# Rotary attention: which heads and queries one step takes, and how often its products are issued

## The reference, cut to what matters

```python
q = (x @ Wq + bq).reshape(B, S, H, Dh).transpose(0, 2, 1, 3)
k = (x @ Wk + bk).reshape(B, S, H, Dh).transpose(0, 2, 1, 3)
...
q, k = apply_rope(q, rope), apply_rope(k, rope)
attn = softmax(q @ k^T / sqrt(Dh))
out = (attn @ v) @ Wo + bo
```

## Time and profile before

| | before |
|---|---|
| median of 3 runs (lowest to highest) | 1888.64 us (1888.54 to 1892.25) |
| span of the profiled execution | 1890.9 us |
| PE busy | 1733.5 us (92%) |
| ACT busy | 1271.8 us (67%) |
| first to last start of an exponential of this layer | 1250.4 to 1777.8 us |

### The profile page before, as it was taken

The page is one execution under the profiler, slowest core; times in us unless marked ns, Lnnn a source line. Parts: engine busy times, 40 slices in busy tenths (PEclk is TensorE's granted clock), DMA queues, the critical chain, the costliest instruction groups (busy, mean ns, idle before and its releaser), DMA issues. The chain is left out here.

```text
span 1890.9 us, 25427 instructions
## 1 busy us (share of the span) xinstructions
PE 1733.5 (92%) x8942; PEld 831.3 (44%) x8942; DVE 1139.3 (60%) x1868; ACT 1271.8 (67%) x2447; POOL 942.0 (50%) x566
## 2 busy tenths in 40 slices
PE   7888579999999999999999999889999999898975
PEld 3433255545555555555454554224333333332354
DVE  5887897986678876688766667332414123120296
ACT  2122115776777678676877777678898998999823
POOL 3555306788876788767888677840000000000033
PEclk9999699999999999999999999889999999999988
DMA  3000000000000000000000000130212212211001
GB/s 85 1 11 1 1 24 11 22 22 11 21 11 22 11 22 22 12 22 11 22 12 21 11 21 5 41 122 24 94 63 69 88 45 68 76 37 37 1 12 36
DMA packets 27863, 59.04 MB, mean 31 GB/s; under 512 B 3840, under 2 KB 14800, under 8 KB 27728
## 3 DMA queue, kind: packets, MB, share of 16 engines
q1 hardware_dynamic: 27728, 57.32, 9.5%
HBM read 38.44 MB, written 18.87 MB: 30 GB/s over the span
## 5 line engine op out<-in xcount | busy, mean ns | idle before, releaser
L894 POOL TENSOR_TENSOR b_psum<-b_psum,b_probs 128x1024 f32<-128x1024 f32 x192 | 463.8, 2416 | 154.2 <-ACT b_probs L1036 147.6
L2308 ACT ACTIVATE c_probs<-banks 128x1024 f32<-128x1024 f32 x512 | 483.5, 1030 | 47.9 <-PE banks L2357 36.8
L1381 DVE TENSOR_TENSOR b_gated<-banks,b_g 128x480 f32<-128x480 f32 x512 | 313.5, 654 | 199.8 <-PE banks L1141 187.7
L1036 ACT ACTIVATE b_probs<-banks 128x1024 f32<-128x1024 f32 x256 | 254.2, 1018 | 212.0 <-PE banks L1174 211.1
L1141 PE MATMUL banks<-b_w,b_xh 128*128 128x480 f32 x1024 | 351.8, 397 | 32.0 <-issue 14.3
L1389 DVE TENSOR_REDUCE b_tok<-b_gated 128x192 f32<-128x960 f32 x256 | 281.4, 1138 | 0.5
L1007 ACT ACTIVATE b_share<-b_o,b_picked 128x64 f32<-128x64 f32 x1080 | 268.7, 337 | 1.5 <-DVE b_o L1414 1.5
L1174 PE MATMUL banks<-b_qq,b_kk 64*128 64x512 f32 x1024 | 261.7, 623 | 1.1 <-DVE b_gated L1381 0.9
L2372 PE MATMUL banks<-c_probs,c_vg 128*32 128x512 f32 x2048 | 250.3, 606 | 2.9 <-DVEq L2423 2.6
L1206 PE MATMUL banks<-b_probs,b_tok 128*64 128x512 f32 x1024 | 249.2, 607 | 2.2 <-ACT b_probs L1036 2.2
L1141 PEld LDWEIGHTS banks<-b_w,b_xh 128*128 128x128 f32 x1024 | 193.6, 189 | 114.0 <-issue 45.9
(11 more groups left out here) (248 smaller groups left out, 1886.3 us busy)
## 6 DMA issues: line engine op xcount, KB each, us to landing
b_raw_w<-in_L_ffn_W SPq DMA_DIRECT2D x32, 480.0 KB, 3.3
c_heads<-c_split SPq DMA_DIRECT2D x24, 512.0 KB
c_keys<-c_heads SPq DMA_DIRECT2D x16, 512.0 KB, 3.7
c_queries<-c_heads SPq DMA_DIRECT2D x16, 512.0 KB, 4.7
c_heads<-c_split SPq DMA_DIRECT2D x8, 384.0 KB
a_xs<-in_L_attn_x SPq DMA_DIRECT2D x4, 512.0 KB, 8.2
out<-d_yo SPq DMA_DIRECT2D x3, 512.0 KB, 3.2
c_heads<-c_split SPq DMA_DIRECT2D x8, 128.0 KB
```

Source lines behind the costliest of these rows:

```text
L894: nc.gpsimd.tensor_tensor(psum[:, par, :], prev, probs[:, i % 4, :], ALU.add).then_inc(psum_rdy, 1)
L1036: nc.scalar.activation(probs[:, i % 4, :], score_b[i % 2], ACT.Exp).then_inc(exp_rdy, 1)
L1381: nc.vector.tensor_tensor(shape(gated[:, t % 2, j, :]), shape(proj_b[u % WAYS][:, 0:HALF_W]), g.unsqueeze(2).broadcast_to([P, 3, HD2, E]), ...
L2308: nc.scalar.activation(probs[:, step % 4, c, :, :], unit_b[u % NU], ACT.Exp, scale=float(HD) ** -0.5).then_inc(exp_rdy, 1)
```

## The change

A step now takes all four heads of a group and one half of the 1,024 queries, where it took two heads and both halves. A unit is still two matmuls of 512 queries and an exponential of 128 x 1024; unit 0 holds heads 0 and 1 of the group, unit 1 heads 2 and 3. The sums in `acc_b` are of four heads and one half of the queries. The products of a step are issued at the next step, at every step, and those of two steps no longer together. The division after the turn becomes one VectorE operation of 4 x 32 elements where there were two of 8 x 8.

```diff
@@ score_unit
-                g, pp, kt = i // STEPS, i // NT % (G // 2), i % NT
+                g, half, kt = i // STEPS, i // NT % 2, i % NT
...
                 for s in range(2):
-                    at = 32 * (2 * pp + s)
-                    last = nc.tensor.matmul(unit_b[u % NU][:, s, :], keys[at:at + 32, par, kt * P:(kt + 1) * P], queries[at:at + 32, par, c * HALF:(c + 1) * HALF], start=True, stop=True)
+                    at = 32 * (2 * c + s)
+                    last = nc.tensor.matmul(unit_b[u % NU][:, s, :], keys[at:at + 32, par, kt * P:(kt + 1) * P], queries[at:at + 32, par, half * HALF:(half + 1) * HALF], start=True, stop=True)
                 last.then_inc(score_ps, 1)
@@ products
-                for s in range(2):
-                    for half in range(2):
-                        at = 64 * s + 32 * half
-                        last = nc.tensor.matmul(acc_b[at:at + 32, :], vg[par][:, kt, 2 * pp + s, :], probs[:, kt % 4, half, s, :],
-                                                start=(kt == 0), stop=(kt == NT - 1))
+                for hh in range(G):
+                    at = 32 * hh
+                    last = nc.tensor.matmul(acc_b[at:at + 32, :], vg[par][:, kt, hh, :], probs[:, kt % 4, hh // 2, hh % 2, :],
+                                            start=(kt == 0), stop=(kt == NT - 1))
@@ batch
                     score_unit(step, 1)
                     if step + 1 < B * BS:
                         score_unit(step + 1, 0)
-                    if i % 2 == 0 and step:
-                        for back in (2, 1):
-                            products(*((b, i - back) if i else (b - 1, BS - back)))
+                    if step:
+                        products(*((b, i - 1) if i else (b - 1, BS - 1)))
                     if i % NT == TURN and not (first and i == TURN):
@@ after the last step
-            for back in (2, 1):
-                products(B - 1, BS - back)
+            products(B - 1, BS - 1)
@@ normalize
-                for s in range(2):
-                    at = pair * 2 * HD + s * HD
-                    o = ao[:, :, at:at + HD].rearrange("p (f j) c -> p f j c", f=2)
-                    nc.vector.tensor_tensor(o, t5[:, s, :, :, 0:HD], recip[:, s, :, :].unsqueeze(3).broadcast_to([P, 2, 4, HD]), ALU.mult).then_inc(ao_rdy, 1)
+                o = ao[:, 4 * half:4 * half + 4, g * G * HD:(g + 1) * G * HD].rearrange("p j (h c) -> p j h c", h=G)
+                nc.vector.tensor_tensor(o, sums[:, :, :, 0:HD], recip.unsqueeze(3).broadcast_to([P, 4, G, HD]), ALU.mult).then_inc(ao_rdy, 1)
```

More of the change, by code:

```diff
@@ L2317, in piece @@
                 if turned:
-                    pe.wait_ge(ao_rdy, ONE + 2 * turned)
+                    pe.wait_ge(ao_rdy, ONE + turned)
                 pe.wait_ge(used, index)
@@ L2322, in piece @@
                 if kind == "turn_out" and half == 0:
-                    pe.wait_ge(ao_rdy, ONE + 2 * NP * (b + 1))
+                    pe.wait_ge(ao_rdy, ONE + NP * (b + 1))
                 if kind in ("q", "q_sw", "k", "k_sw"):
@@ L2355, in score_unit @@
                 for s in range(2):
-                    at = 32 * (2 * pp + s)
-                    last = nc.tensor.matmul(unit_b[u % NU][:, s, :], keys[at:at + 32, par, kt * P:(kt + 1) * P], queries[at:at + 32, par, c * HALF:(c + 1) * HALF], start=True, stop=True)
+                    at = 32 * (2 * c + s)
+                    last = nc.tensor.matmul(unit_b[u % NU][:, s, :], keys[at:at + 32, par, kt * P:(kt + 1) * P], queries[at:at + 32, par, half * HALF:(half + 1) * HALF], start=True, stop=True)
                 last.then_inc(score_ps, 1)
             def products(b, i):
-                par, pp, kt, pair = i // STEPS % 2, i // NT % (G // 2), i % NT, i // NT
+                par, kt, pair = i // STEPS % 2, i % NT, i // NT
                 pe.wait_ge(exp_rdy, ONE + 2 * (b * BS + i) + 2)
@@ L2380, in turn @@
                 pe.wait_ge(used, index)
-                pe.wait_ge(ao_rdy, ONE + 2 * n)
+                pe.wait_ge(ao_rdy, ONE + n)
                 for j in range(4):
@@ L2475, in normalize @@
                 dve.wait_ge(accT_ps, n + 1)
-                t5 = piece_b.rearrange("p (j s f c) -> p s f j c", j=4, s=2, f=2)
-                recip = own_recips[:, n * 2 * NT:(n + 1) * 2 * NT].rearrange("p (s f j) -> p s f j", s=2, f=2)
-                nc.vector.reciprocal(recip, t5[:, :, :, :, HD]).then_inc(recip_rdy, 1)
+                g, half = pair // 2, pair % 2
+                sums = piece_b.rearrange("p (j h c) -> p j h c", j=4, h=G)
+                recip = own_recips[:, n * 2 * NT:(n + 1) * 2 * NT].rearrange("p (j h) -> p j h", h=G)
+                nc.vector.reciprocal(recip, sums[:, :, :, HD]).then_inc(recip_rdy, 1)
                 dve.wait_ge(recip_rdy, n + 1)
-                for s in range(2):
-                    at = pair * 2 * HD + s * HD
-                    o = ao[:, :, at:at + HD].rearrange("p (f j) c -> p f j c", f=2)
-                    nc.vector.tensor_tensor(o, t5[:, s, :, :, 0:HD], recip[:, s, :, :].unsqueeze(3).broadcast_to([P, 2, 4, HD]), ALU.mult).then_inc(ao_rdy, 1)
+                o = ao[:, 4 * half:4 * half + 4, g * G * HD:(g + 1) * G * HD].rearrange("p j (h c) -> p j h c", h=G)
+                nc.vector.tensor_tensor(o, sums[:, :, :, 0:HD], recip.unsqueeze(3).broadcast_to([P, 4, G, HD]), ALU.mult).then_inc(ao_rdy, 1)
             dve.wait_ge(used, NX)
```

## The result

The changed kernel takes 1898.62 us (median of 4 runs, 1897.92 to 1900.35), the kernel before on the same chip 1889.96 (1888.54 to 1892.25). The ratio is 1.0044, 95% interval 1.0029 to 1.0058: 8.7 us slower, where 9 us less were forecast. A second set of runs on another chip gave 1.0042 (1.0029 to 1.0055).

A forecast was written before the change was run, and what follows sets the result against it. ScalarE's exponentials were taken to bound the rotary layer, needing 462.5 us plus waits. Waits of 56.7 against 64.9 gain 8.2, with the end 9.1; span 1881.8, median 1879.5 us. Range 1865 to 1890, 1875 to 1885 at 0.52.

The forecast's parts named there:

- The loop: Two steps without a piece: four exponentials' dependency cycle falls from 3.90 to 3.04 us, under ScalarE's 3.62, regaining 0.28.
- Products 0.99, score units 0.43: On TensorE, 8 product instructions take 0.99 us; two score units back to back take 0.43, before 0.66.
- Pieces: Extra TensorE work between steps: 0.59 just hidden, 1.02 loses 0.35, 1.09 up to 0.51, tail projection 3.65 us.
- Chains: VectorE's work after a _sw piece delays the copy of the sums at five places, losing 2.36 us each.
- The norms: Layer norms on VectorE delay the copy: 4.05, 4.08, 4.08, 2.78 us lost in batches 0 to 3, plus 1.5 each.
- The small terms: Short losses across the layer: 0.59 pieces just hidden, 1.02 pieces 0.35 us, boundaries with short pieces 0.25.
- the start: First exponentials of the layer: first products wait until 1257.62, the clock is low, and 5.6 us are lost.
- the boundaries: Between groups of 8 steps, where the sums are copied: 0.25 us with short pieces, 1.13 with 1.02 pieces on both sides.
- From the span to the time: Whole kernel: span falls from 1890.9 to 1881.8 us, and the runs' median stands 2.3 lower, giving 1879.5.
- the sign: Whole kernel's time: faster at chance 0.74, within 0.2% at 0.13, slower at 0.13.
- the waits at the copies take all: Rival, chance 0.13: in five chains TensorE stands about 1.5 us, costing the clock; gain only 1.6, 1887 us.
- Slower: Rival, chance 0.13: two score units back to back stay at 0.66 us, costing 28 us more, 1908 us.

The follow-up runs named there:

- e13: Four heads per step, norms moved as in e9, but products issued every step where there are no pieces; ratio 0.9859 to the kernel before, 1869.38 us.
- e9: Changed kernel with products of two steps issued together and VectorE's layer norms moved behind a copy of the sums; ratio 0.9929 to the kernel before, 1877.64 us.
- e18: Changed kernel with GpSimd's addition moved to the fourth group except in batch 0, clear of all norms; ratio 1.0006 to the kernel before, 1894.67 us.
- e3: Changed kernel with the first products of each 8 steps issued one step later, with the second ones; ratio 1.0119 to the kernel before, 1911.68 us.

## Why the prediction was wrong

The mechanisms were named rightly, and the sum of what ScalarE loses, 56.7 us, was 16.3 too small (73.0). The four norms hold 6.8 of that, many small terms 9.5.

- *The loop*, 3.90 to 3.04 and so hidden under 3.62: right. 0.917 per exponential in batch 3, and e13 against e9 shows its worth.
- *Products 0.99, score units 0.43*: right as sizes, with one limit. Where the second unit still waits for an exponential that has just started again after a stall, the pair takes 0.61 or more, not 0.43.
- *Pieces*: under-sized. I took 0.35 for a 1.02 piece in a row. ScalarE's timeline of the changed kernel, two periods of four exponentials with such a piece in each:

```profile
1443.36 3.77 ACT L2308 ACTIVATE c_probs<-banks 128x1024 f32<-128x1024 f32 x4 [0.33 <-PE banks L2357]
1447.47 3.77 ACT L2308 ACTIVATE c_probs<-banks 128x1024 f32<-128x1024 f32 x4 [0.33 <-PE banks L2357]
```

  The period is 1447.47 - 1443.36 = 4.11, so 0.49 is lost on the 3.62, though only 0.33 of it shows as idle.
- *Chains*: right in place and cause, 2.1 idle and about 0.5 just before, 2.7 where 2.36 were forecast.
- *The norms*: the first step that failed. "VectorE is busy 1427.74 - 1418.68 = 9.06" was carried over from the old schedule and came to 11.12 in batch 1 (1420.47 to 1431.59), since GpSimd's addition, which just missed the norm before, fell into it; in batches 2 and 3 it grew by 1.96 and 2.00. Over twelve exponentials each, as the forecast counts them, the four norms lose 6.0, 7.9, 7.7 and 6.2 us, 27.8 together, where 21.0 were forecast with the 1.5 of low clock in each. In e18, without the addition in them, they lose 19.5: the rest of this step, low clock included, was sized well in sum.
- *The small terms*: the second. Turns without a piece and short pieces were taken as "just hidden" (0.59 on 0.58), and a turn loses about 0.2, some 1.6 in all. The steps ahead of the norms lose 0.4 more in each of three batches, the five chains 1.6 more, the start 0.9; the other 4 or so are the 1.02 pieces and the boundaries. Each is small beside its period, but there are dozens of them, against a gain of 8.2.
- *From the span to the time*: the forecast put the median 2.3 us below the span, as in the kernel before; the changed kernel's lies 2.3 above. That is 4.6 of the 19.1 us between 1879.5 and 1898.6, and no part of the mechanism.
- Which step made what: with the addition out of the norms, e18 still loses 64.2 against the 64.9 of before and its time is that of before. So the small terms ate the gain, and the longer norms turned no change into a slower kernel. With a forecast gain of 8.2 out of terms of 57 and 65, the sign was not mine to give at 0.74.
- *Rivals*: "the waits at the copies take all" was nearest in kind, but put its extra cost at the chains and stopped at no change; in the changed kernel the clock did not fall behind a chain. "Slower" named the score units, which held. The slower case that came true, a longer norm, was not among them.

## What to carry to other kernels

When work that waits on a single buffer is issued more finely, the copy that frees the buffer loses its slack. List what stands ahead of that copy on its engine, and move it or keep the coarse order just there. A net gain that is the difference of two large sums of stalls deserves a wide range, and a duration read from one schedule is not one of the other if a second engine's work shifts beside it. Many terms taken as "just hidden" deserve a size of their own. Try the halves of a combined change alone: here one was worth 9 us, and the other, added to it, lost 17.

## What the runs showed of the hardware

- A VectorE operation of 0.34 us (128x128 f32 from SBUF to SBUF) took 2.36 to 2.38 when it started 0.05 to 0.12 us behind GpSimd's addition of 128x1024 (2.40 us); in batch 1 of the changed kernel VectorE's next operation started at 1428.80, as the addition ended. In the kernel before, an operation of the same kind that was already running when the addition began took its usual 0.34, and so did the copies from the banks beside it, 0.69 and 0.68. The Trainium skill (GPSIMD Engine Reference, Key points) says that GpSimd shares its SBUF interfaces with VectorE and contends with its instructions in a 2-port mode or with two SBUF inputs; the traces show such a contention, but not in which mode the operation ran, and the page has no price for it.
- The granted clock fell to 0.50 without any long wait of TensorE: in e3, behind a step of score units alone with two waits of 0.42 us, nine times in a layer.
- The exponentials' median duration in the profile rose from 1.025 us to 1.057, while their starts came closer, 0.917 apart in batch 3; the duration is no measure of what one costs.
